# Row scatters of a GpSimd queue, each held back until ScalarE's next exponent

## What is computed

```
x = x + _L0_attn_ref(_layernorm(x, axis=-1), ...)              # Mamba scan
x = x + _L0_xattn_ref(_layernorm(x, axis=-1), ctx_768, ...)    # 16 heads, softmax over the context
x = x + _L0_ffn_ref(_layernorm(x, axis=-1), ...)               # top 2 of 8 experts
x = x + _L1_attn_ref(...); x = x + _L1_xattn_ref(...); x = x + _L1_ffn_ref(...)
```

## Time and profile before

| | us |
|---|---|
| median of 3 runs | 1459.77 |
| lowest and highest run | 1448.18, 1461.08 |
| span of the profiled execution, first to last instruction | 1552.4 |
| PE busy in it | 1214.8 |
| VectorE, ScalarE, GpSimd busy | 1011.3, 902.7, 771.3 |

### The profile page before, as it was taken

The page is one execution under the profiler, slowest core; times in us unless marked ns, Lnnn a source line. Parts: engine busy times, 40 slices in busy tenths (PEclk is TensorE's granted clock), DMA queues, the critical chain, the costliest instruction groups (busy, mean ns, idle before and its releaser), DMA issues. The chain is left out here.

```text
span 1552.4 us, 31341 instructions
## 1 busy us (share of the span) xinstructions
PE 1214.8 (78%) x11210; PEld 936.1 (60%) x11218; DVE 1011.3 (65%) x2376; ACT 902.7 (58%) x1718; POOL 771.3 (50%) x590
## 2 busy tenths in 40 slices
PE   6898989898768887675599938998699886538882
PEld 2666766676564665454499935666356664428772
DVE  5999999999997786555111117886379675433334
ACT  3988898889744886442355527776366453213333
POOL 1999999998954123444355531110113243346552
PEclk8999999999999998766699979999799787659996
DMA  5241222122000311111688732000200001047665
GB/s 191 84 143 55 111 84 84 56 111 84 28 1 8 56 40 31 51 34 55 198 246 257 231 79 55 15 16 16 75 2 25 24 26 35 29 146 208 204 204 174
DMA packets 98028, 138.51 MB, mean 89 GB/s; under 512 B 13965, under 2 KB 77402, under 8 KB 93684
## 3 DMA queue, kind: packets, MB, share of 16 engines
q1 hardware_dynamic: 85764, 117.08, 25.3%
q0 software_dynamic: 9088, 17.07, 3.2%
q10 hardware_dynamic: 3024, 2.36, 0.5%
HBM read 105.91 MB, written 28.19 MB: 86 GB/s over the span
## 5 line engine op out<-in xcount | busy, mean ns | idle before, releaser
L353 POOL TENSOR_TENSOR M_dbx<-M_u,M_b_sb 128x1024 f32<-128x1024 f32 x127 | 296.8, 2364 | 33.2 <-DVE M_e L440 15.5
L454 DVE TENSOR_TENSOR_SCAN M_h<-M_pA,M_dbx 128x512 f32<-128x512 f32 x256 | 298.2, 1207 | 6.5 <-ACT M_pA L612 6.2
L612 ACT ACTIVATE M_pA<-M_dt,M_a_neg 128x504 f32<-128x504 f32 x256 | 175.0, 684 | 21.7 <-DVE M_h L454 17.4
L2159 POOL DMA_INDIRECT F_slots<-F_line,F_pos x128 | 127.1, 993 | 54.4 <-issue 37.9
L2532 PE MATMUL X_bank<-F_xT,F_wbuf 128*128 128x256 f32 x624 | 152.4, 388 | 0.0
L1864 PE MATMUL X_bank<-L_ident,X_s_sb 128*128 128x128 f32 x512 | 94.6, 312 | 69.7 <-ACT X_pt_sb L1727 63.0
L622 ACT ACTIVATE M_hc<-M_pT,M_cT 128x256 f32<-128x256 f32 x256 | 119.8, 469 | 42.9 <-PE M_pT L759 41.5
L1727 ACT ACTIVATE X_pt_sb<-X_bank 128x512 f32<-128x512 f32 x128 | 76.3, 596 | 105.7 <-PE X_bank L1864 105.4
L1552 DVE TENSOR_REDUCE X_smax<-X_bank 128x8 f32<-128x512 f32 x128 | 82.3, 685 | 82.7 <-PE X_bank L1855 80.9
L775 PE MATMUL M_pY<-M_ident,M_hc 128*128 128x128 f32 x1024 | 135.1, 275 | 0.4
L775 PEld LDWEIGHTS M_pY<-M_ident,M_hc 128*128 128x128 f32 x1024 | 125.0, 192 | 0.3
(11 more groups left out here) (339 smaller groups left out, 2810.1 us busy)
## 6 DMA issues: line engine op xcount, KB each, us to landing
M_b_sb<-M_rows_bc SPq DMA_DIRECT2D x32, 1024.0 KB, 4.7
F_wbuf<-in_F_wcat SPq DMA_DIRECT2D x39, 578.0 KB
F_wbuf<-in_F_wcat SPq DMA_DIRECT2D x39, 450.0 KB
X_s_sb<-F_slots SPq DMA_DIRECT2D x39, 132.0 KB
F_xblk<-F_slots SPq DMA_DIRECT2D x39, 132.0 KB
F_line<-F_line SPq DMA_DIRECT2D x16, 256.0 KB
S_ya<-F_answers SPq DMA_DIRECT2D x16, 256.0 KB, 5.7
F_slots<-F_pad ACTq DMA_DIRECT2D x16, 132.0 KB
```

The lines of the kernel that those rows point to most:

```text
L353: pool.tensor_tensor(dbx[:, k % DBXS, :, :], u[:, g % 2, :, :], bc(b_sb[:, n, :], 1, 2), ALU.mult).then_inc(dbx_ready, 1)
L454: v.tensor_tensor_scan(h[:, k % STATES, half, :], pA[:, (2 * k + half) % DECAYS, :, :].rearrange("p b t -> p (b t)"), dbx[:, k % DBXS, hal ...
L612: act.activation(pA[:, (2 * k + half) % DECAYS, :, 1:SEQ], dt[:, g % 2, half, :].rearrange("p (b t) -> p b t", t=SEQ)[:, :, 1:SEQ], ACT.Ex ...
L2159: pool.indirect_dma_start(slots, bass.IndirectOffsetOnAxis(pos[:, g, k, t:t + 1], 0), line[:, g % RING, k, t, :], None, bounds_check=E * C ...
```

## The change

`pool_scatter` gets a wait ahead of each of its two transfers: `exp_done` of the attention must have reached the number that stands after ACT's first exponent of the step (for the first transfer) or its second one (for the second), cut at 64, the number after the last exponent. The two semaphores are handed out of `attention_stage`, and the 14 becomes a name. Nothing else is moved.

```diff
     st.o_used, st.y_done, st.xnT_ready, st.ot_ready, st.q_ready = o_used, y_done, xnT_ready, ot_ready, q_ready
+    st.s_psum, st.exp_done = s_psum, exp_done
...
+    FIRST_SCATTER = 14
...
         for a in (2 * n, 2 * n + 1):
+            pool.wait_ge(att.exp_done, min(2 * (FIRST_SCATTER + g * PER + n) - 1 + a % 2, 2 * STEPS))
             k, t = a // TILES, a % TILES
             pool.indirect_dma_start(slots, bass.IndirectOffsetOnAxis(pos[:, g, k, t:t + 1], 0),
...
-                g, n = (i - 14) // PER, (i - 14) % PER
+                g, n = (i - d.FIRST_SCATTER) // PER, (i - d.FIRST_SCATTER) % PER
...
-                if 14 <= i < STEPS and in_range(g):
+                if d.FIRST_SCATTER <= i < STEPS and in_range(g):
```

More of the change, by code:

```diff
@@ L2056, in dispatch_stage @@
     st.slots, st.table, st.weight = slots, table, weight
+    st.FIRST_SCATTER = FIRST_SCATTER
     pM = bank[:, 6, :]
```

## The result

| | before | changed |
|---|---|---|
| median of 20 runs each, us | 1450.8 (1445.9 to 1461.1) | 1463.0 (1459.2 to 1466.9) |
| ratio, 95% interval | | 1.0072 [1.0053, 1.0092] |
| span of the recorded execution, us | 1552.4 | 1465.0 |

The account below looks back on a forecast made before the run. Bound: ScalarE and VectorE stall on PE's signals while GpSimd issues many transfers back to back, 89.2 us in the recorded execution. Timed runs were taken as stall-free: 1459.8 + 6.0 = 1465.8, so 1466 us; range 1430 to 1476.

Parts of the forecast that it names:

- the runs have no stalls: Likeliest case: timed runs have no stalls or few, only the attention's end costs; 1466 us, 1460 to 1471, chance 0.58.
- The recording itself makes the stalls: Both attentions: recording makes or lengthens the stalls behind rows of transfers, 89.2 us, which timed runs do not have.
- The sum 1552.4 - 89.2 = 1463.2: Recorded span less both attentions' stalls (38.7 us layer 0, 50.5 layer 1), 3 us from the runs' median.
- the stall-free 1448.9 us: Span without attention stalls and layer 1's 14.3 us of expert-part idling, matched to 1460 - 12 = 1448 us for the runs.
- if the span falls by 80 us and the time stays, the stalls belong to the recording: Sign for the whole kernel: recorded span down 80 us with unchanged timed runs would show that the recording makes the stalls.
- the runs have all of it: Rival: timed runs hold all 89.2 us of the attentions' stalls, so the change gives 1377 us; chance 0.12.
- A pair costs nothing: Inside the attention: two transfers in a row cause no stall, so spacing gives back 89.2 us in a recorded execution.
- groups of 22 us at clock 1.00 from 584 on: Sign in layer 0's attention of the changed kernel's trace: groups take 22 us at full granted clock from 584 on.
- The stalls of the tail's unspaced row: Sign at the attention's end: the eight-in-a-row stalls stay, while "remote" rows fall from 76 to under 25 us.
- The end: Attention's end: held transfers delay group 6's `pool_normal` by 2.7 us in layer 0, 3.3 in layer 1; +6.0 us, 0 to 11.2.
- slower: Rival at the attention's end: paced transfers also delay group 6's first pair and group 7's `pool_normal`; 16 us, 1476 us, chance 0.08.
- Inside the loop: Attention's steps: `pool_normal` may start 0.2 us later, in layer 1 about 1 us, additions have slack; cost 0.

Follow-up runs that it names:

- longer rows: Kernel before with four more indirect transfers in each of groups 0 to 3, ten in a row: 1454.3 us (0.9989) on chip 2, 1610.3 us (1.034) on chip 5.
- end waits only: Kernel before with the new waits only on group 4's last four transfers (steps 32 and 33), on chip 2: 1461.2 us, ratio 1.003.
- the loop's waits alone: Changed kernel with the new waits only on transfers of steps 14 to 31, on chip 2: 1458.5 us, ratio 1.0031 to before.
- the kernels with half of the waits: Two kernels on chip 2 against before: new waits only on steps 14 to 31, 1458.5 us; only on steps 32 and 33, 1461.2 us.

## Why the prediction came out right, and where it was wrong

**The time.** 1466 us against 1463.0, span 1469 against 1465.0: the likeliest case ("the runs have no stalls") held for the chip that was timed. The closeness is in part luck. The forecast adds 6.0 us to 1459.8, the median of three runs; 20 runs of before have 1450.8. The starting point was 9 us too high and the cost 4 to 6 us too low (10.4 by the ratio, 12.2 by the medians), and the two cancel. Two of its reasons did not hold either.

**"The recording itself makes the stalls": wrong.** The sum 1552.4 - 89.2 = 1463.2 came near the runs, and its meaning was not right. Of the 87.4 us that the span lost, the two attentions gave 67.6 us (table above), where 89.2 less 6.0 were forecast, and 18.7 came from layer 1's expert part, which the change does not touch. The 92.6 us between the recorded and the timed executions of before were read as recorded against not recorded. By all signs they were one kind of chip against another: with its span of 1552.4, its "remote" rows and its missing landing times the recording belongs with chip 9's (1562.6, of runs at 1559). A run here is longer than its span by only 1.8 us (1466.85 for the changed kernel's 1465.0), not by the 12 of the prediction's estimate, so the stall-free 1448.9 us had no such support. The sign that I named, "if the span falls by 80 us and the time stays, the stalls belong to the recording", came true and still could not tell the two apart. A second recording of before was needed. The rival "the runs have all of it" (chance 0.12) is what happens on chips 9 and 5. There the gain is 49 us and not 83. "A pair costs nothing", from the earlier trace rows, does not hold in full there: at clock 1.00 a group of layer 1 with pairs takes 23.4 us on chip 9, 22.8 in the first recording of the changed kernel, and the groups after it 24.5 to 27.5 at 0.93 to 0.81 against 21.2 at 1.00. Chip 9's changed kernel also keeps the 20 us of the expert part.

**Signs that did not come.** The prediction asked for groups of 22 us at clock 1.00 from 584 on; in layer 0 three of four were slower, at 0.66 to 0.81. The stalls of the tail's unspaced row were to stay, and they were gone too. Both stood in the changed kernel's first recording, and the second one pointed away from "the spacing removed the stalls": where nothing was spaced, nothing stalled either.

**The end: right in kind, 6.0 us forecast.** VectorE's waits for the row root rose from 3.8 us (four waits in before) to 12.4, so 8.6 us. 8.1 of them are group 6's. The term was short since the first of the last three transfers starts 0.80 us after exponent 64's end (687.28 against 686.48), where I had it back to back, so that the row root starts 4.3 us behind that end, not 2.5 to 3.5. Nor is it the end waits' alone. A wait of 2.08 and 2.07 us for group 6's row root is there without them: the transfers held back in the loop make the queue late, a part that the forecast put at 0 and only the rival "slower" named. Part of the 3.8 was itself measured beside stalls; the unstalled trace with longer rows has 5.5.

**Inside the loop: not quite 0.** GpSimd's queue did hold up the additions, onto VectorE's copies (744 to 1029 ns), and a group of layer 0 at full clock takes 22.3 us with the waits and 21.9 without (end waits only). The third group takes 28.79 us at 0.70 in the changed kernel and 28.78 at 0.70 with the loop's waits alone, but 25.90 at 0.80 with the end waits alone. These are single recordings; the kernels with half of the waits cost about 4.5 us each.

**The clock goes with it.** Over 35 runs of before on chip 2, time and mean granted clock go together, from 1445.6 us at 0.930 to 1464.4 at 0.912, about 1 us for each 0.001. The changed kernel's runs have a median of 0.915, those of before on chip 2 0.922. By that line the lower clock alone stands for some 7 of the 10.4 us, so it overlaps with the waits above and is not a further term. In one place both meet. The stretch 1250.90 to 1276.35 takes 25.45 us at 0.80; with the end waits alone it is as slow, and without them quick:

```profile
1253.80:1280.72 26.92, 21.70 (x291) 17.74 (x285) 15.99 (x55) 11.10 (x20) 11.06 (x13) 0.81 0.11 34
```

```profile
1251.15:1270.67 19.52, 14.94 (x225) 11.96 (x225) 14.59 (x53) 10.49 (x19) 11.03 (x12) 1.00 0.16 50
```

In part the stretch is longer because the row root that closes it starts later. The lower clock there (1.2 GHz for part of the group) comes in the recordings of both kernels with end waits, and neither in this one without them nor in that with longer rows (19.24 us at 1.00). The prediction had no term for that. What it adds to the waits' own 8 us was not separated.

## What to carry to other kernels

A recorded execution that is longer than every timed run has to be recorded again, unchanged, before a cause is given to the gap: here the chip is what fits. A median of three runs was itself 9 us off. A chain of GpSimd's indirect transfers can be free on one chip and cost some 80 of 1557 us on another (the rest of the 100 us between them lies in an expert part that the chain does not touch), so a change that spaces them out should be timed on both kinds; it lost 0.7% on one and won 3.2% on the other. Holding a queue back with waits costs where the queue has no idle time left, which was at the end of each attention, and what was held back in the last steps of the loop counts there too.

## What the runs showed of the hardware

- Two kinds of chip: with the same program and the same rows on GpSimd, ScalarE and VectorE wait for PE on chips 9 and 5 while indirect transfers start 1.28 us apart (before takes 1558 and 1557 us), and PE's own small matmuls come in pieces there (2.55 us for eight). On chip 2 neither is seen (1454 us, eight in 1.06 us); for chip 0 there are the times of before (1456 us) and a recording at 1.7 us apart. Inside the attention each transfer in a row adds 1.42 us to the release, for rows of four, six, eight and ten. What causes it, why only some chips show it, and whether it is the chip or the time at which it came up, no run here tells.
- Memsets between the transfers (1.47 us apart, not 1.28) bring the release of a row of six from 8.8 us down to 5.3 to 6.8 in layer 0 on chip 5, and leave it at 8.2 to 9.0 in layer 1.
- The Trainium skill, "SBUF — State Buffer", section "Who interferes with whom", says that PE and ACT never wait on anyone. Chip 9's rows show ScalarE idle 12.2 us behind a row of transfers on GpSimd, so as an account of what such a row costs others the rule does not hold there; as an account of ports alone no run here tests it.
- The same section says that a VectorE instruction with two inputs in SBUF contends with a GpSimd instruction that reads SBUF, and that the order of issue decides who waits. The trace agrees with the first: predicated copies of 744 ns take 1029 on average (1074 on chip 9) once GpSimd's additions fall beside them, and 742 again when these are moved. The second no run here tests.
